# The second-choice additions at the ends of two expert layers, moved from VectorE to GpSimd

## The chip, the cores and the metric

The kernel runs on one core of one Trainium2 chip. The metric is the device time of one execution in microseconds, of which the median over several runs is taken. A profiled execution gives, beside its own time, a trace of every instruction; its span reaches from the first to the last instruction on the core.

## What is computed

The program is one forward pass of four residual layers over an input of 2 x 1024 tokens with 128 features: differential attention, a mixture of experts, attention with a decaying state, and the same mixture of experts again. Only the expert layer bears on this change:

```python
logits = xf @ router_w.T                       # 8 experts
scores = softmax(logits)
topk_scores, topk_ids = top_k(scores, 2)
topk_scores = topk_scores / topk_scores.sum(-1, keepdims=True)
for each expert (wg, wu, wd, w):
    h = silu(xf @ wg) * (xf @ wu)
    acc = acc + w[:, None] * (h @ wd)          # w is 0 but for the two chosen
x = x + acc
```

In words: x becomes x plus the first choice's result times its weight plus the second choice's result times its weight.

## The kernel before

`X` is the running x in on-chip memory: 128 partitions by 16 tiles of 128 values, fp32. It stays there through all four layers. Each layer writes one instruction list per engine inside a `Block`. At the end of a block every engine drains and meets the others at a barrier (L1234 in the records), after which GpSimd clears the semaphores (L2257 after the first expert layer, L2269 after the second) and a second barrier lets the next block begin.

`moe` is that expert layer, built twice: tag `m1` (after the first attention) and tag `m2` (the end of the program). It does not run every expert over every token. The tokens are sorted by expert into 39 slots of 128 rows. For each slot GpSimd gathers 128 rows with an indirect DMA (`gather`, L1274), TensorE, ScalarE and VectorE compute the expert's output `ys`, and GpSimd scatters its rows with an indirect DMA to `yd_rows` in HBM (`scatter`, L1280). That is 39 gathers and 39 scatters on GpSimd in a layer.

When all 39 scatters have landed (`results_in`, L1229 to L1232), the rows come back in token order: SyncE loads the first choices' rows, ScalarE's queue the second choices', each in four quarters of 4 tiles, into `GB` (printed `m_GB`; 128 x 512 values in a quarter). Then, by quarters q = 0 to 3:

- ScalarE multiplies the second choice's four tiles in place by their weights (L1407) and counts `weighted`.
- VectorE adds the first choice's four tiles times their weights to `X`, four instructions of 128x128 (L1507), and counts `first_added`.
- VectorE waits for both counts and adds the second choice's quarter to `X`, one instruction of 128x512 (L1513), and counts `summed`.

In the second layer SyncE waits for `summed` and stores each quarter of `X` to the output (L2265); it begins with that only when the first choice's last quarter has been loaded. In the first layer SyncE loads the next layer's weights instead (L2251 to L2254), and the next block begins with VectorE's statistics of `X` (L85).

The order within an engine's list is the order in which the code is written. VectorE's list at the end of the layer is L1507 x 4, L1513, four times over; GpSimd's list ends with the last scatter.

Of the kernel before, what the change touches and what calls it, by code (L numbers as in the profile page):

```python
# [9 lines left out]
ALU = mybir.AluOpType  # L10
# [1146 lines left out]
def moe(nc, tag, X, W3, ident, scratch, norm, route, statistics_done, deviations_done, experts_loaded, prefetch, store=None):  # L1157
# [4 lines left out]
    NQ, TQ = 4, 4  # L1162
# [7 lines left out]
    with ExitStack() as ctx:  # L1170
        def sb(name, shape, dt=F32):
            return ctx.enter_context(nc.sbuf_tensor(f"{tag}_{name}", shape, dt))
# [4 lines left out]
        def sems(names):  # L1177
            return [nc.alloc_semaphore(f"{tag}_{name}") for name in names.split()]
# [26 lines left out]
        GB = sb("GB", [P, NQ, 2, TQ, P])  # L1205
# [15 lines left out]
        weighted, first_added, summed = sems("weighted first_added summed")  # L1221
        NCONST = 8

        def quarter(q):
            return slice(TQ * q, TQ * q + TQ)
# [8 lines left out]
        with nc.Block() as block:  # L1234
            @block.sync
            def _(sp):
                for q in range(NQ):
                    sp.wait_ge(xn_ready, TQ * q + TQ)
                    sp.dma_start(XD[q * TQ * P:(q + 1) * TQ * P, :].rearrange("(t p) d -> p t d", p=P), XN[:, quarter(q), :])\
                      .then_inc(xn_stored, 16)  # L1240
                results_in(sp, 0)

                sp.wait_ge(gathered[NQ - 1][0], 16)
                prefetch(sp)
                if store is not None:
                    for q in range(NQ):
                        sp.wait_ge(summed, q + 1)
                        store(sp, q)

            @block.gpsimd  # L1250
            def _(pool):
# [26 lines left out]
                def scatter(s):  # L1278
                    pool.wait_ge(y_copied, s + 1)
                    pool.indirect_dma_start(out=YD[:, :], out_offset=bass.IndirectOffsetOnAxis(  # L1280
                        ap=target[:, s:s + 1], axis=0), in_=ys[:, s % YB], in_offset=None)\
                        .then_inc(ys_stored[s % YB], 16)
# [6 lines left out]
                for s in range(SLOTS):  # L1289
                    if s + XB < SLOTS:  # L1290
                        gather(s + XB)
                    scatter(s)

            @block.tensor
            def _(pe):


                def counts():
                    for t in range(NT):
                        nc.tensor.matmul(RC[:, (t + 1) * E:(NT + 1) * E].rearrange("p (t e) -> p t e", e=E), ones[:],  # L1300
                                         M[:, t:t + 1].to_broadcast([P, NT - t, E]), start=(t == 0), stop=False)
                        last = nc.tensor.matmul(RC[:, t * E:(t + 1) * E], tri[:], M[:, t], start=False, stop=(t == NT - 1))
                    last.then_inc(rc_done, 1)

                pe.wait_ge(const_c, 3)
                counts()

                order = [c for c in range(PC) if c >= PC // 2] + [c for c in range(PC) if c < PC // 2]
                for m, c in enumerate(order):
                    pe.wait_ge(placed, m + 1)  # L1310
                    planes = 3 if c >= PC // 2 else 2
                    for i in range(PI):
                        last = nc.tensor.matmul(IV[:, 0:planes * SLOTS].rearrange("p (a s) -> p a s", a=planes),  # L1313
                                                place_oh[:, c, :, i], marks[:, c, 0:planes, :, i],
                                                start=(m == 0 and i == 0), stop=(m == PC - 1 and i == PI - 1))
                last.then_inc(iv_done, 1)
                pe.wait_ge(experts_loaded, 48)

                def x_turn(s):
                    pe.wait_ge(xs_loaded[s % XB], s // XB * 16 + 16)  # L1320
                    if s:
                        pe.wait_ge(xt_copied, s)
                    nc.tensor.transpose(XT[:, 0:P], xs[:, s % XB], ident[:]).then_inc(xt_done, 1)  # L1323

                def up(s):
                    pe.wait_ge(w_copied, s + 1)
                    pe.wait_ge(xt_copied, s + 1)
                    for k, H, done in ((0, GP, g_done), (1, UP, u_done)):  # L1330
                        for j in range(FK):
                            last = nc.tensor.matmul(H[:, s % 2, j * P:(j + 1) * P], wgu[:, s % 2, k, j * P:(j + 1) * P],  # L1332
                                                    xt[:, s % 2], start=True, stop=True)
                        last.then_inc(done, 1)

                def down(s, e):
                    pe.wait_ge(h_ready, s + 1)
                    if s:
                        pe.wait_ge(y_copied, s)
                    for j in range(FK):  # L1340
                        last = nc.tensor.matmul(YP[:, 0:P], hs[:, s % 2, j * P:(j + 1) * P],  # L1341
                                                WD[:, bass.ds(e, 1), j, :].rearrange("p o d -> p (o d)"),
                                                start=(j == 0), stop=(j == FK - 1))
                    last.then_inc(y_done, 1)

                x_turn(0)
                pe.wait_ge(etab_ready, 1)
                up(0)
                x_turn(1)
                for s in range(SLOTS):  # L1350
                    e = pe.value_load(etab[0:1, s:s + 1], min_val=0, max_val=E - 1)
                    if s + 1 < SLOTS:
                        up(s + 1)
                    if s + 2 < SLOTS:
                        x_turn(s + 2)
                    down(s, e)
# [54 lines left out]
            def _(dve):  # L1411
# [92 lines left out]
                for q in range(NQ):  # L1504
                    dve.wait_ge(gathered[q][0], 16)
                    for t in range(TQ * q, TQ * q + TQ):
                        last = nc.vector.scalar_tensor_tensor(out=X[:, t, :], in0=GB[:, q, 0, t % TQ],  # L1507
                                                              scalar=wts[:, 0, t:t + 1], in1=X[:, t, :], op0=ALU.mult,
                                                              op1=ALU.add)
                    last.then_inc(first_added, 1)  # L1510
                    dve.wait_ge(weighted, TQ * q + TQ)
                    dve.wait_ge(first_added, q + 1)
                    nc.vector.tensor_tensor(X[:, quarter(q), :], X[:, quarter(q), :], GB[:, q, 1], ALU.add)\  # L1513
                      .then_inc(summed, 1)


def decay_attention(nc, X, ident, weights, LR, norm, route):
# [684 lines left out]
def program(nc, io, out, upto="all"):  # L2202
    NT = 16
    with ExitStack() as ctx:
# [51 lines left out]
        if upto != "attn_a":  # L2256
            with nc.cleanup_on_exit():  # L2257
                moe(nc, "m1", X, W3, ident, scratch, norm, route, NT // 2, 0, experts_loaded, load_decay_weights)
# [9 lines left out]
        if upto == "all":  # L2268
            with nc.cleanup_on_exit():  # L2269
                moe(nc, "m2", X, W3, ident, scratch, norm, route, NT, NT - 2, experts_loaded, lambda sp: None, store_out)  # L2270
# [28 lines left out]
```

## Time and profile before

| | us |
|---|---|
| median of 3 runs | 1130.73 (1129.43 to 1135.28) |
| profiled execution, its own time | 1133.65 |
| its span | 1131.9 |
| TensorE busy | 1006.1 (89%) |
| VectorE busy | 751.6 (66%) |
| ScalarE busy | 743.6 (66%) |
| GpSimd busy | 437.4 (39%) |

Busy times are sums over the span; they say how much an engine works, not which of them sets the end at a given place. The change touches two stretches, of some 8 us each, in which TensorE has nothing to do: the end of the first expert layer (about 632 to 641 us) and the end of the second, which is the end of the program (about 1121 to 1132 us). What counts there is the order in which loads land and VectorE, ScalarE and later GpSimd follow each other, which a timeline shows, and the barrier behind them, which needs the records of the sequencers (printed DVEq, POOLq, SPq).

### The profile page before, as it was taken

The numbers are of one execution on the slowest core, as the hardware profiler recorded it, in microseconds if no ns is written. First come the engines' busy times: TensorE is split into PE (matmuls) and PEld (weight loads), VectorE is DVE, ScalarE is ACT, GpSimd is POOL, SyncE is SP. The second block draws the span as 40 slices with busy tenths as digits, with TensorE's granted clock in tenths as the row PEclk, the third lists the DMA queues.
The fourth block names the chain that finished last, engine by engine and source line by source line (L and its number), as shares of the span: only waits on it lengthen the run. The fifth ranks groups of instructions, "written<-read, shape, count | busy, mean of one in ns | idle before, by whom it ended". The sixth has DMA issues, their size and how long they took to land. (4 is left out here: it accounts for less than half of the span.)

```text
span 1131.9 us, 26076 instructions
## 1 busy us (share of the span) xinstructions
PE 1006.1 (89%) x9820; PEld 691.3 (61%) x9820; DVE 751.6 (66%) x1519; ACT 743.6 (66%) x1496; POOL 437.4 (39%) x580
## 2 busy tenths in 40 slices
PE   5889999999999999748999489999999999479993
PEld 3333333333333334548999367888888888479993
DVE  7699999999999997882333635656566666443333
ACT  4658888887888887345665366676666666356663
POOL 3752112211122211217764124444444444256761
PEclk9889999999999999968999589999999999779997
DMA  2243111111111100611111422111212110021114
GB/s 71 84 126 100 31 31 49 39 31 30 31 47 42 31 2 3 223 38 48 48 48 36 157 70 76 39 76 39 75 39 68 45 65 12 8 64 49 50 41 126
DMA packets 40033, 64.65 MB, mean 57 GB/s; under 512 B 10024, under 2 KB 21032, under 8 KB 37992
## 3 DMA queue, kind: packets, MB, share of 16 engines
q1 hardware_dynamic: 31736, 50.14, 14.0%
q0 software_dynamic: 4992, 10.23, 3.4%
q10 hardware_dynamic: 3184, 2.63, 0.7%
q8 instruction: 81, 1.33, 0.5%
q14 instruction: 40, 0.33, 0.1%
HBM read 47.86 MB, written 14.68 MB: 55 GB/s over the span
## 5 line engine op out<-in xcount | busy, mean ns | idle before, releaser
L890 ACT ACTIVATE PB<-S 128x512 f32<-128x512 f32 x576 | 307.9, 597 | 71.3 <-PE S L696 66.5
L996 DVE TENSOR_REDUCE mx<-S 128x2 f32<-128x1024 f32 (+1 forms) x192 | 207.5, 1127 | 7.6 <-PE S L682 7.6
L958 POOL TENSOR_SCALAR_AFFINE_SELECT PB<-PB 128x512 f32<-128x512 f32 x128 | 79.0, 635 | 306.9 <-ACT PB L890 306.8
L731 PE MATMUL PV<-PB,VP 128*32 128x256 f32 (+2 forms) x2432 | 177.7, 379 | 0.0
L1489 DVE TENSOR_TENSOR m_hs<-m_gs,m_UP 128x512 f32<-128x512 f32 x78 | 53.7, 689 | 159.3 <-ACT m_gs L1380 157.2
L696 PE MATMUL S<-W 50*128 50x512 bf16 (+3 forms) x768 | 123.9, 328 | 4.9 <-ACT PB L890 4.2
L682 PE MATMUL S<-W 48*128 48x512 bf16 (+3 forms) x640 | 94.4, 326 | 13.4 <-DVE mx L992 4.9
L1280 POOL DMA_INDIRECT yd_rows<-m_ys,m_target x78 | 76.6, 981 | 59.9 <-DVE m_ys L1496 59.9
L1274 POOL DMA_INDIRECT m_xs<-xn_rows,m_source x78 | 75.8, 972 | 48.1 <-DVE m_source L1469 24.9
L731 PEld LDWEIGHTS PV<-PB,VP 128*32 128x32 f32 x2432 | 51.6, 108 | 69.1 <-issue 59.4
L682 PEld LDWEIGHTS S<-W 48*128 48x128 bf16 x640 | 26.8, 94 | 108.3 <-issue 44.7
L1332 PE MATMUL m_GP<-m_xt,m_wgu 128*128 128x128 f32 x624 | 84.8, 280 | 1.8 <-ACT m_xt L1376 1.8
L986 DVE TENSOR_REDUCE mx<-S 128x8 f32<-128x1024 f32 x64 | 78.3, 1223 | 11.6 <-PE S L675 11.2
L1332 PE MATMUL m_UP<-m_xt,m_wgu 128*128 128x128 f32 x624 | 84.1, 279 | 0.0
L1341 PE MATMUL m_YP<-W,m_hs 128*128 x624 | 82.6, 275 | 1.2 <-DVE m_ys L1496 1.2
L1386 ACT ACTIVATE m_wgu<-W 128x1024 f32 x78 | 82.6, 1058 | 1.4 <-issue 1.3
L1376 ACT ACTIVATE m_xt<-m_XT 128x128 f32<-128x128 f32 x78 | 21.6, 277 | 91.5 <-PE m_XT L1323 91.5
L1868 ACT ACTIVATE d_enegs<-d_PA 128x512 f32<-128x512 f32 x64 | 37.8, 590 | 64.6 <-PE d_PA L1667 60.2
L1332 PEld LDWEIGHTS m_GP<-m_xt,m_wgu 128*128 128x128 f32 x624 | 77.8, 196 | 3.1 <-issue 3.1
L1901 ACT ACTIVATE d_DM<-d_LQ,d_nL 128x128 f32<-128x128 f32 x252 | 78.1, 387 | 0.0
L1332 PEld LDWEIGHTS m_UP<-m_xt,m_wgu 128*128 128x128 f32 x624 | 77.7, 196 | 0.0
L1341 PEld LDWEIGHTS m_YP<-W,m_hs 128*128 128x128 f32 x624 | 75.8, 192 | 1.6 <-issue 1.6
(311 smaller groups left out, 1947.5 us busy)
## 6 DMA issues: line engine op xcount, KB each, us to landing
d_LQ<-l_rows SPq DMA_DIRECT2D x15, 1024.0 KB, 4.7
W<-qk_parts SPq DMA_DIRECT2D x210, 32.0 KB
qk_parts<-OT SPq DMA_DIRECT2D x24, 256.0 KB, 3.0
W<-qk_parts SPq DMA_DIRECT2D x30, 96.0 KB
W<-in_L_ffn_w_gate SPq DMA_DIRECT2D x1, 2048.0 KB, 9.3
W<-in_L_ffn_w_up SPq DMA_DIRECT2D x1, 2048.0 KB, 14.6
xn_rows<-m_XN SPq DMA_DIRECT2D x8, 256.0 KB, 2.3
m_GB<-yd_rows SPq DMA_DIRECT2D x8, 256.0 KB, 5.5
```

The costliest lines, as they stand in the source:

```text
L682: ins = nc.tensor.matmul(S1[:, b, a, 256 * k:256 * k + w], QS[base:base + KR, s, h, qb * P:(qb + 1) * P], KS[base:base + KR, s, h, c * 512 ...
L696: ins = nc.tensor.matmul(S2[:, j % 3, col:end], KS[base:base + KM, s, h, kb * P:(kb + 1) * P], QS[base:base + KM, s, h, q0:q0 + end - col] ...
L731: ins = nc.tensor.matmul(PV[32 * u:32 * u + 32, shift + col:shift + end], VP[:, g, kb, u // 2, :], PB[:, slot, col:end], start=(kb == 0 an ...
L890: nc.scalar.activation(PB[:, j % NPB, :], S2[:, j % 3, :], ACT.Exp, scale=SC).then_inc(exp_done, 1)
L958: nc.gpsimd.affine_select(out=tri, in_=tri, compare_op=ALU.is_ge, fill=0.0, base=0, pattern=[[0, U], [1, P]], channel_multiplier=-1).then_ ...
L986: nc.vector.reduce_max(mx[:, g % 2, 2].rearrange("p a h q -> p (a h) q")[:, :, q:q + 2], S1[:, b].rearrange("p a (h j k) -> p (a h) j k", ...
L996: nc.vector.reduce_max(mx[:, g % 2, c, :, heads[0], qb], S1[:, b, :, 0:w], AX.X)\
L1280: pool.indirect_dma_start(out=YD[:, :], out_offset=bass.IndirectOffsetOnAxis(ap=target[:, s:s + 1], axis=0), in_=ys[:, s % YB], in_offset= ...
L1332: last = nc.tensor.matmul(H[:, s % 2, j * P:(j + 1) * P], wgu[:, s % 2, k, j * P:(j + 1) * P], xt[:, s % 2], start=True, stop=True)
L1341: last = nc.tensor.matmul(YP[:, 0:P], hs[:, s % 2, j * P:(j + 1) * P], WD[:, bass.ds(e, 1), j, :].rearrange("p o d -> p (o d)"), start=(j ...
L1386: nc.scalar.activation(wgu[:, s % 2], W3[:, 0:2 * n].rearrange("p (k e f) -> p k e f", k=2, e=E) [:, :, bass.ds(e, 1), :].rearrange("p k o ...
L1901: last = nc.scalar.activation(DM[:, i, j % 2, j // 2], LQ[:, b, h], ACT.Exp, bias=nL[:, t, h:h + 1])
```

## The change

The addition of the second choice's quarter leaves VectorE's list and is written at the end of GpSimd's, after the last scatter, with the same two waits and the same count. It is done in both expert layers, four additions each.

```diff
                     scatter(s)
 
+                for q in range(NQ):
+                    pool.wait_ge(weighted, TQ * q + TQ)
+                    pool.wait_ge(first_added, q + 1)
+                    nc.gpsimd.tensor_tensor(X[:, quarter(q), :], X[:, quarter(q), :], GB[:, q, 1], ALU.add)\
+                      .then_inc(summed, 1)
+
             @block.tensor
...
                     last.then_inc(first_added, 1)
-                    dve.wait_ge(weighted, TQ * q + TQ)
-                    dve.wait_ge(first_added, q + 1)
-                    nc.vector.tensor_tensor(X[:, quarter(q), :], X[:, quarter(q), :], GB[:, q, 1], ALU.add)\
-                      .then_inc(summed, 1)
```

VectorE, end of the second layer, before (`m_hs` is the gated hidden value of a slot, `m_ys` the slot's output; from the third row on the end of the layer; two more pairs like the last two rows follow):

```order
L1489 TENSOR_TENSOR m_hs<-m_gs,m_UP 128x512
L1496 COPY m_ys<-m_YP 128x128 x2
L1507 SCALAR_TENSOR_TENSOR X<-m_GB,m_wts,X 128x128 x4
L1513 TENSOR_TENSOR X<-X,m_GB 128x512
L1507 SCALAR_TENSOR_TENSOR X<-m_GB,m_wts,X 128x128 x4
L1513 TENSOR_TENSOR X<-X,m_GB 128x512
```

VectorE at the same place, after (the diff shifts the line numbers by 6):

```order
L1502 COPY m_ys<-m_YP 128x128
L1495 TENSOR_TENSOR m_hs<-m_gs,m_UP 128x512
L1502 COPY m_ys<-m_YP 128x128 x2
L1513 SCALAR_TENSOR_TENSOR X<-m_GB,m_wts,X 128x128 x16
L1234 UNCONDITIONAL_BRANCH
```

VectorE's sixteen weighted additions now stand in one run, with waits only for the loads of their quarters.

GpSimd, end of the first layer, before (L1234 leaves the block, with its drain and barrier; L2257 clears the semaphores; L68 and L1596 belong to the next layer):

```order
L1274 DMA m_xs<-xn_rows,m_source 128x128
L1280 DMA yd_rows<-m_ys,m_target 9088x128 x9
L1234 UNCONDITIONAL_BRANCH
L2257 ISA
L68 UNCONDITIONAL_BRANCH
L1596 MEMSET d_ones 128x128
```

GpSimd at the same place, after:

```order
L1274 DMA m_xs<-xn_rows,m_source 128x128
L1280 DMA yd_rows<-m_ys,m_target 9088x128 x9
L1297 TENSOR_TENSOR X<-X,m_GB 128x512 x4
L1234 UNCONDITIONAL_BRANCH
L2259 ISA
L68 UNCONDITIONAL_BRANCH
L1598 MEMSET d_ones 128x128
```

The four additions stand between the last scatter and the block's end, so that GpSimd's drain comes behind them and no longer directly behind the last indirect DMA. At the end of the second layer its list changes in the same way. The lists of TensorE, ScalarE and SyncE are the same as before.

## Rows read from the trace of the kernel before

**Rows 1.** Page: the span, and the chain that ended last by engine

```profile
span 1131.9 us, 26076 instructions
...
PE 10%; DVE 1%; DMA 1%; POOL 0%; issue 0%; ACT 0%; POOLq 0%; DVEq 0%; ACTq 0%
```

**Rows 2.** Timeline, end of layer 2: start, duration, engine, line, operation [idle before]

```profile
1114.87 0.96 POOL L1280 DMA_INDIRECT yd_rows<-m_ys,m_target  x1 [0.78 <-DVE m_ys L1496]
1117.24 1.76 SPq L1232 DMA_DIRECT2D m_GB<-yd_rows  x4
...
1121.43 1.14 DVE L1507 SCALAR_TENSOR_TENSOR X<-m_GB,m_wts,X 128x128 f32<-128x128 f32 x4 [6.83 <-DMA m_GB<-yd_rows]
1121.63 2.55 ACT L1407 ACTIVATE m_GB<-m_GB,m_wts 128x128 f32<-128x128 f32 x8 [10.26 <-DMA m_GB<-yd_rows]
1122.94 0.69 DVE L1513 TENSOR_TENSOR X<-X,m_GB 128x512 f32<-128x512 f32 x1 [0.38 <-ACT m_GB L1407]
...
1126.18 1.28 ACT L1407 ACTIVATE m_GB<-m_GB,m_wts 128x128 f32<-128x128 f32 x4 [0.18 <-DMA m_GB<-yd_rows]
...
1128.48 0.69 DVE L1513 TENSOR_TENSOR X<-X,m_GB 128x512 f32<-128x512 f32 x1
```

**Rows 3.** Timeline, end of layer 1 and first work behind it

```profile
632.80 1.14 DVE L1507 SCALAR_TENSOR_TENSOR X<-m_GB,m_wts,X 128x128 f32<-128x128 f32 x4 [6.76 <-DMA m_GB<-yd_rows]
...
636.27 2.44 ACT L1407 ACTIVATE m_GB<-m_GB,m_wts 128x128 f32<-128x128 f32 x8 [0.60 <-DMA m_GB<-yd_rows]
...
639.90 0.69 DVE L1513 TENSOR_TENSOR X<-X,m_GB 128x512 f32<-128x512 f32 x1
...
641.63 3.19 DVE L85 BATCH_NORM_STATS2 d_ln_stats<-X 128x6 f32<-128x128 f32 x16 [1.04 <-PEq L2257]
```

**Rows 4.** Layer 2, first choice's loads of quarters 1, 2, 3: issue to landing

```profile
DMA to landing us min/median/max: 5.0/5.0/5.0
...
DMA to landing us min/median/max: 6.3/6.3/6.3
...
DMA to landing us min/median/max: 7.4/7.4/7.4
```

**Rows 5.** Three lines' instructions: duration ns min/median/max, first and last start, shapes

```profile
L1507 DVE SCALAR_TENSOR_TENSOR X<-m_GB,m_wts,X x32: 343/346/351, 632.8 to 1128.0; 128x128 f32<-128x128 f32 x32
...
L969 POOL TENSOR_TENSOR PB<-VP,rs x7: 1057/1060/1567, 467.7 to 483.0; 128x512 f32<-128x512 f32 x7
...
L1067 DVE TENSOR_TENSOR VP<-VP,y x16: 424/424/787, 431.8 to 477.5; 128x256 f32<-128x256 f32 x16
```

**Rows 6.** Timeline, two places where VectorE and GpSimd work at once

```profile
474.12 1.06 POOL L969 TENSOR_TENSOR PB<-VP,rs 128x512 f32<-128x512 f32 x1 [0.31 <-PE S L761]
...
474.67 0.79 DVE L1067 TENSOR_TENSOR VP<-VP,y 128x256 f32<-128x256 f32 x1
...
482.98 0.69 DVE L1126 TENSOR_TENSOR PB<-VP,rs 128x512 f32<-128x512 f32 x1
483.02 1.57 POOL L969 TENSOR_TENSOR PB<-VP,rs 128x512 f32<-128x512 f32 x1 [7.84 <-DVE rs L1085]
```

**Rows 7.** Drains at block ends: ns min/median/max, first and last start

```profile
L1234 POOLq DRAIN  x2: 7629/7638/7647, 626.1 to 1114.6; - x2
L1234 DVEq DRAIN  x2: 698/700/703, 639.9 to 1128.5; - x2
...
L1234 SPq EVENT_SEMAPHORE  x2: 17/17/17, 640.8 to 1129.9; - x2
...
L607 POOLq DRAIN  x1: 1674/1674/1674, 483.0 to 483.0; - x1
```

**Rows 8.** The last scatter's flight (chain), SyncE's last wait (waits), scatters (page)

```profile
1114.87 2.23 DMA yd_rows<-m_ys,m_target
...
SPq L2271 <- DMA out_x<-X: 0.8, 1, 0.8
...
L1280 POOL DMA_INDIRECT yd_rows<-m_ys,m_target x78 | 76.6, 981 | 59.9 <-DVE m_ys L1496 59.9
```

## The prediction, made before the changed kernel was run

> **What bounds the kernel now.** I began with the page: TensorE is busy for 89% of 1131.9 us, and the chain that ended last lies mostly on it [rows 1]. That says nothing of this change, since TensorE is idle at both places that the diff touches. So I went to the timeline of each place, then to the landing times of the loads, then to rows where GpSimd and VectorE work at once, and last to the drains and barriers that close each block.
>
> The reader should see three things. First, the end of layer 2 is VectorE's: from 1121.43 it runs four rounds of 1.14 us (L1507 x 4) and 0.69 us (L1513), and the last addition ends at 1128.48 + 0.69 = 1129.17; it waited for ScalarE only once, 0.38 us [rows 2]. ScalarE's weighting ends at 1126.18 + 1.28 = 1127.46, 1.7 us sooner. Layer 1 has the same shape, 632.80 to 640.59 [rows 3]. Second, behind the last addition stands a barrier. The engines pass it at 640.8 and 1129.9 [rows 7]; statistics of X follow at 641.63 [rows 3], and in layer 2 the clearing of semaphores and SyncE's wait for the last output store, 0.8 us [rows 8]. Third, GpSimd's drain at that barrier takes 7.63 and 7.65 us [rows 7]. It starts at 626.1 and 1114.6 and ends at about 633.75 and 1122.25, long before VectorE is done, so that today it costs nothing.
>
> **The additions themselves.** VectorE loses 8 instructions of 0.69 us, 5.5 us in all. GpSimd gains 8 two-input fp32 operations of 128x512; L969 is the same kind and shape, 1.06 us undisturbed [rows 5]. If nothing disturbed them, the last one would start when ScalarE's last weight is done, 1127.46 + 0.05 = 1127.51, and end at 1128.57: 0.60 us sooner than 1129.17. In layer 1 ScalarE ends at 636.27 + 2.44 = 638.71 [rows 3], the addition at 639.82, 0.77 us sooner. Together -1.4 us.
>
> But the two engines get in each other's way when both read two inputs from on-chip memory. L1067 takes 0.42 us as a rule and 0.79 us at its longest, which is where L969 is under way: L969 ends at 475.18 and L1067 at 475.46, 0.28 us behind it. The other way round, L969 takes 1.57 us when L1126 started 0.04 us before: L1126 ends at 483.67, L969 at 484.59, 0.92 us behind it [rows 5, 6]. So one waits until the other is done, and saves only some 0.14 us of its start. L1507 reads X and GB, the additions too. The Trainium skill, page "SBUF — State Buffer", section "Who interferes with whom", gives this as a rule: a VectorE instruction with two SBUF inputs and a GpSimd instruction that reads SBUF share an interface, and the second blocks until the first is done. By that rule, too, the case is not the -1.4 us of free running but the walk below; the trace agrees, with 0.37 and 0.51 us of waiting.
>
> The walk for layer 2, with loads of quarters 1 to 3 issued at 1117.6, 1118.1 and 1118.6 and landing at 1122.7, 1124.4 and 1126.0 [rows 2, 4]: VectorE begins quarter 1 at 1122.70. GpSimd is ready at 1122.96, when L1513 is today, gets in behind an instruction of VectorE and ends at 1124.02. An L1507 alone takes 0.35 us and four take 1.14 [rows 2, 5], so they start 0.26 apart; held up, the first ends 0.35 - 0.14 = 0.2 us after GpSimd. VectorE's three left end at 1124.02 + 0.20 + 2 x 0.26 = 1124.75. GpSimd's second addition follows VectorE's next instruction (until 1125.01) and ends at 1125.93; VectorE 1126.66 (its loads are there since 1124.4); third addition, again behind one instruction of VectorE, 1127.84; VectorE 1128.57; the last one, alone, 1128.62 to 1129.68. That is 0.5 us later than 1129.17. If VectorE's runs of four are never broken up, the same terms give 1129.6 to 1129.8. Fully one behind the other, 4 x 1.14 + 4 x 1.06 from 1121.43 with 0.2 us of handshakes, it is 1130.4, +1.2. The low end is the -0.6 above. I take +0.5 in either layer: last additions end at 1129.68 and 641.08.
>
> **The drain.** This is where the sum is decided. GpSimd's drain at L607 ends with the work before it: it starts at 483.0, takes 1.67 us and ends 0.1 us after L969, 484.59 [rows 6, 7]. The two of 7.6 us stand directly behind the indirect DMAs. The last of these is issued by 1114.87 + 0.96 = 1115.83 and has landed at 1117.10 [rows 2, 8], yet the drain ends at 1122.25, 5.15 us later, and the two differ by 18 ns. Nothing else in the profile lasts until then. I read it as work that the drain does itself once a block has indirect DMAs behind it: 39 gathers and 39 scatters in a layer [rows 8], and 7.63 / 78 is 98 ns for each. Behind the additions this work begins 14 us later than today, where nothing covers it: VectorE, ScalarE and SyncE wait at the barrier for GpSimd.
>
> Its price: a drain starts about 0.2 us before the instruction ahead of it runs (1114.6 against 1114.87). With the last addition from 1128.62 it would end at 1128.4 + 7.64 = 1136.1. From below: only the 5.15 us behind a landed DMA are its own, 1129.68 + 5.15 = 1134.8. From above: the whole 7.64 begins when the addition ends, 1137.3. I take 1136.1, which agrees with counting from the end of issue (1115.83 to 1122.25, 6.4 us). Against the barrier at 1129.85 this is +6.25; SyncE's 0.8 us for the last store are then covered, so +5.45 (4.2 to 6.7). In layer 1 the drain ends at 639.8 + 7.64 = 647.45, against 640.6 for VectorE's drain (639.9 + 0.70): +6.85 (5.6 to 8.1). Nothing that follows makes it up, as the next block needs X and the barrier.
>
> **Sum:** 5.45 + 6.85 = 12.3 us (9.8 to 14.8), with the lock's 0.5 us a layer in it. On the profiled execution that is 1133.65 + 12.3 = 1145.9. That execution lies 2.9 us above the median, which is scatter between runs (1129.43 to 1135.28), so I put the difference on the median: 1130.73 + 12.3 = 1143.0.
>
> **Rival 1, not slower: the drain is hidden.** Its 7.6 us run from the last indirect DMA, wherever the drain stands (entries taken off the ring while GpSimd waits, say). They would be over at 1122.25, before the first addition at 1122.96, and likewise in layer 1. For it: the drain at L607 has no work of its own. The Trainium skill's page "PSUM — Partial Sum Buffer", section "Engine vs sequencer instructions", says that a drain waits for its engine to be fully idle, and no more. By that rule GpSimd's drain would end with the last addition, and the time be as here; the 5.15 us after a landed DMA are not explained by it. Against: GpSimd stands idle 1.8 us of each 2.8 us round in the slots and could have cleared its backlog there. What remains is the lock, +0.5 us twice: 1131.7 us (up to 1133.1 if all is serial).
>
> **Rival 2, faster: free running.** Drain hidden, and the weighted additions do not block: -1.4, 1129.4 us. Rows 6 speak against it.
>
> **Rival 3, slower still:** the whole drain after the addition in both layers, plus serial additions (0.7 a layer more): 14.8 + 1.4, 1147 us.
>
> **Chances.** A measurement of this kernel can tell about 0.5%, 5.7 us. Drain exposed 0.58 (forecast 1143.0, own range 1139.5 to 1146.5), rival 3 0.05, rival 1 0.29, rival 2 0.06; 0.02 for a gain above 0.5% that I see no way to. So faster 0.02, same 0.35, slower 0.63. As the second case holds more than 0.2, the range must reach it: 1130.0 to 1147.0.
>
> **What would show it.** In the profile after: GpSimd's drain at L1234 (7.6 us, beginning near 640 and 1128) and the first statistics behind layer 1 near 648.5 instead of 641.63: the drain is right. A drain of about 1 us there and statistics near 642: rival 1. Additions of 1.06 us and weighted additions of 0.35 us all through: no lock; one of them near 1.2 us or an L1507 above 1 us: the lock. The last output store should be issued near 1129.7 in both cases; its landing would no longer end the program if the drain does. The forecast fails if the 7.6 us are bound to the last indirect DMA and not to the drain.

## The result, and the profile after

The changed kernel takes 1149.74 us (median of 4 runs, 1148.56 to 1152.25). The kernel before, run beside it, takes 1132.62 us (median of 4, 1129.43 to 1135.28; the three runs shown ahead are among them). The ratio is 1.0154, with a 95% interval of 1.013 to 1.0179: 14.7 to 20.3 us slower. The forecast was slower, by 12.3 us, and its range ended at 1147.0, 2.7 us too low.

The page of the changed kernel shows a span of 1146.8 us and, but for GpSimd's 10 us more, busy times within 1.3 us of those before. VectorE's is no shorter although 5.5 us of additions have left it, since an instruction that is held up counts as busy:

```profile
span 1146.8 us, 26076 instructions
...
PE 1006.1 (88%) x9820; PEld 691.8 (60%) x9820; DVE 752.9 (66%) x1511; ACT 743.7 (65%) x1496; POOL 447.8 (39%) x588
```

Busy times do not tell where the time went. The timeline of layer 1's end does (start, duration, engine, line, operation, idle time before it); it answers to [rows 3]:

```profile
629.16 1.14 DVE L1513 SCALAR_TENSOR_TENSOR X<-m_GB,m_wts,X 128x128 f32<-128x128 f32 x4 [6.78 <-DMA m_GB<-yd_rows]
...
630.51 6.38 DVE L1513 SCALAR_TENSOR_TENSOR X<-m_GB,m_wts,X 128x128 f32<-128x128 f32 x12 [0.20 <-DMA m_GB<-yd_rows]
630.78 1.27 POOL L1297 TENSOR_TENSOR X<-X,m_GB 128x512 f32<-128x512 f32 x1 [7.15 <-ACT m_GB L1413]
...
632.87 1.26 POOL L1297 TENSOR_TENSOR X<-X,m_GB 128x512 f32<-128x512 f32 x1 [0.82 <-DVE X L1513]
...
634.95 1.26 POOL L1297 TENSOR_TENSOR X<-X,m_GB 128x512 f32<-128x512 f32 x1 [0.82 <-DVE X L1513]
...
637.03 1.26 POOL L1297 TENSOR_TENSOR X<-X,m_GB 128x512 f32<-128x512 f32 x1 [0.82 <-DVE X L1513]
...
646.12 3.19 DVE L85 BATCH_NORM_STATS2 d_ln_stats<-X 128x6 f32<-128x128 f32 x16 [9.23 <-PEq L2259]
```

The last addition ends at 638.29, 9.13 us after the first weighted addition began; before it was 7.79. Then 7.8 us pass in which no engine does anything, until the statistics start. What fills them is in the records of the barrier (name, count, ns min/median/max, first and last start), which answer to [rows 7]:

```profile
L1234 DVEq DRAIN  x2: 3367/3409/3451, 633.5 to 1134.3; - x2
L1234 SPq DRAIN  x2: 122/123/124, 636.4 to 1139.5; - x2
L1234 POOLq DRAIN  x2: 7737/7744/7750, 637.0 to 1137.7; - x2
L1234 SPq EVENT_SEMAPHORE  x2: 17/17/17, 645.2 to 1145.6; - x2
```

GpSimd's drain starts with the last addition (637.0) and ends at 644.8, 6.46 us behind the end of that addition. SyncE passes the barrier at 645.2. Layer 2 is the same: 1137.7 + 7.74 = 1145.4, barrier at 1145.6.

The kernel can be cut into stretches that are compared one by one: from the first weighted addition of layer 1 to the first statistics behind it (end 1), from there to the first weighted addition of layer 2, and from there to the end of the span (end 2).

| us | end 1 | end 2 | sum over before |
|---|---|---|---|
| before | 8.83 | 10.47 | |
| before, on the second chip | 8.84 | 10.46 | |
| changed | 16.96 | 16.77 | 14.4 |
| changed, second profile | 16.94 | 16.93 | 14.6 |
| early drain | 10.47 | 11.82 | 3.0 |
| late drain, additions on VectorE | 15.42 | 15.70 | 11.8 |
| drain in the middle as well | 12.96 | 12.83 | 6.5 |
| first layer only | 16.87 | 10.50 | 8.1 |
| second layer only | 8.83 | 16.80 | 6.3 |

The two ends repeat within 0.2 us from profile to profile, on two chips. They are the measure of the mechanism. The rest of the program, which the change does not touch, moves as well: in the changed kernel's profile the stretch ahead of end 1 is 3.6 us shorter than before (629.16 against 632.80) and the one between the ends 4.1 us longer. With the 14.4 us of the ends that makes the 14.9 between the two spans.

### The profile page after: what moved, and what is told of

It reads as the page before. It is cut to its first block and busy times, and to the rows that moved or that the text cites. A ratio compares the mean times of both kernels' runs of the same rounds, so it can differ in the third digit from the quotient of the medians.

```text
span 1146.8 us, 26076 instructions
## 1 busy us (share of the span) xinstructions
PE 1006.1 (88%) x9820; PEld 691.8 (60%) x9820; DVE 752.9 (66%) x1511; ACT 743.7 (65%) x1496; POOL 447.8 (39%) x588
## 6 DMA issues: line engine op xcount, KB each, us to landing
W<-in_L_ffn_w_up SPq DMA_DIRECT2D x1, 2048.0 KB, 14.6
```

## The experiments

**The changed kernel once more**, for scatter.

> The changed kernel once more, beside the others on the same chip, to tell which part of the +17 us is the two ends of the layers and which part is the clock elsewhere. Theory: ends of the layers cost 8.1 us (first weighted addition of layer 1 to first statistics behind it: 8.83 us before, 16.96 in the changed kernel) and 6.3 us (first weighted addition of layer 2 to the end: 10.47 and 16.77); the 4.1 us more between them go with TensorE's granted clock (0.97 against 0.99 there) and change from run to run. Rival: those 4.1 us come again in each run, as a longer idle stretch in front of the third layer keeps the clock low for longer.

Measured: ratio 1.0136 (1.0102 to 1.0169) to 1134.49 us, so 11.6 to 19.2 us slower; ends 16.94 and 16.93 us. The additions took 1.26 us again. So what the ends lose is the change's, 14.5 us of the 17.1 in the first comparison. The 4.1 us between the ends came again here (483.8 us against 479.8), which by itself would speak for the rival; the kernel before once more, at the end of this section, shows how far.

**An early drain.** One more drain, directly behind the last scatter, in the changed kernel:

```diff
                     scatter(s)
+                nc.gpsimd.drain()
 
                 for q in range(NQ):
                     pool.wait_ge(weighted, TQ * q + TQ)
```

> The changed kernel with one more GpSimd drain directly behind the last scatter, ahead of the four additions, in both layers. Theory (the drain works through the indirect DMAs behind it, once): the added drain takes 7.6 us, ends near 7.4 us after the last scatter's start, some 0.7 us before the first addition is ready, and so costs nothing; the drain at the block's end then takes only as long as the last addition, about 1.3 us. What is left of the loss is the additions on GpSimd: 1.34 us in layer 1, 1.23 in layer 2 by the two traces, plus 0.3 for a barrier that GpSimd reaches last: 2.5 to 3.5 us slower than before, 1135 us against 1132. Rival (a drain behind a block with indirect DMAs always costs its 6.4 us, whatever drains stood before): the block's drain stays at 7.7 us and the kernel at +15 to +17 us. Rival (the GpSimd additions themselves make the drain long): the added drain is short, the last one stays long, +15 to +17 us.

Measured: ratio 1.004 (1.002 to 1.006) to 1134.49 us, 2.3 to 6.8 us slower. L1293 is the added drain, L1234 the one at the block's end:

```profile
L1293 POOLq DRAIN  x2: 7637/7642/7647, 623.3 to 1114.9; - x2
```

```profile
L1234 POOLq DRAIN  x2: 1349/1349/1349, 637.9 to 1129.2; - x2
```

The 7.64 us have moved to the new drain, which ends at 631.0 and 1122.5, before the first additions (631.70 and 1122.95). The last drain is as long as the addition ahead of it and 0.09 us more. The ends lose 1.6 and 1.35 us instead of 8.1 and 6.3. Both rivals fall: the work is done once, and it is not the additions that make it.

**A late drain alone.** The kernel before, with one wait more on GpSimd; all additions stay on VectorE:

```diff
                     scatter(s)
+                pool.wait_ge(summed, NQ)
```

> The kernel before, all additions on VectorE; GpSimd only waits at the end of its list until all four quarters are summed, so that its drain begins when VectorE is done. Theory (late drain alone makes the loss): GpSimd's drain begins near the last addition's end and takes 6.4 to 7.7 us; the barrier comes 6.5 to 7.5 us later in layer 1, and the program's end 5.5 to 6.5 us later in layer 2 (0.8 us of the wait for the last store is covered): +12 to +14 us against before, and the additions on VectorE stay at 0.69 us. Rival (the loss comes from the additions on GpSimd and the lock between the engines): +0 to +1 us. Rival (the drain's work is over while GpSimd waits): drain under 0.2 us, +0 to +0.5 us.

Measured: ratio 1.0076 (1.005 to 1.0103), 5.7 to 11.7 us slower. The ends lose 6.6 and 5.2 us, 11.8 together: a little below the 12 to 14 that I wrote, as nothing but the drain's own work is left in it. The whole time moved by less than I expected too, and its interval ends just under what the ends lose. The drain alone, with no instruction of GpSimd under way ahead of it:

```profile
L1234 POOLq COMPARE_BRANCH  x2: 38/38/38, 642.0 to 1137.1; - x2
L1234 POOLq DRAIN  x2: 6414/6421/6428, 642.2 to 1137.2; - x2
```

VectorE's last addition starts at 641.29 and takes 0.69 us; GpSimd passes its wait at 642.0, drains until 648.6, and the statistics start at 649.61. So the larger part of the loss needs no addition on GpSimd at all.

**A drain in the middle**, to see what its length hangs on. The changed kernel, with a drain behind scatter 19:

```diff
                     scatter(s)
+                    if s == 19:
+                        nc.gpsimd.drain()
```

> The changed kernel with one more GpSimd drain in the middle of the slots, behind scatter 19 (28 gathers and 20 scatters issued by then, 11 gathers and 19 scatters after it), in both layers; looked at for its drains. Theory (so much for each indirect DMA since the last drain, 6.4 to 7.6 us for 78, 82 to 98 ns each): the drain in the middle takes some 4 to 5 us, the last one 30 x 82 to 98 ns = 2.5 to 2.9 us beyond the end of the last addition. Rival (a fixed time when any indirect DMA lies behind it): both take 6.4 to 7.6 us. The whole time is then that of the changed kernel less up to 4 us a layer at the end, plus what the drain in the middle holds up, which the slots' slack may hide in part.

Measured: one profile, span 1138.7 us. L1294 is the drain in the middle:

```profile
L1294 POOLq DRAIN  x2: 5204/5210/5217, 574.8 to 1067.7; - x2
```

```profile
L1234 POOLq DRAIN  x2: 3812/3812/3812, 640.6 to 1133.5; - x2
```

The last one less the 1.35 us that cover the addition is 2.46 us for 30 indirect DMAs: 82 ns each. The late drain's 6.42 us for 78 are 82 ns each, and the changed kernel's 7.74 - 1.35 = 6.39 as well. The drain in the middle follows 48, 3.94 us at that price, and starts 1.22 us before the scatter ahead of it is issued (574.83 and 576.05): 5.16 us, against 5.20 and 5.22, a little over the 4 to 5 expected. A fixed time is ruled out, and so is a length that grows with the time since the last drain: the late drain starts 16 us later than that of before (642.2 against 626.1) and does the same 6.4 us of work. The drain's length is proportional to the indirect DMAs issued since the last drain. Each of them moves 128 rows, so whether the price is for a DMA or for its rows is not told apart, and what the drain does in that time no trace shows. The drain of before fits too: 0.23 us ahead of the last scatter, 0.96 of its issue and 6.42 make 7.61 us, against 7.63 and 7.65 [rows 2, 7]. In this sum the scatter's landing has no part.

**One layer at a time.** These and the two runs below went to another chip, on which the kernel before takes 1171.1 us (19 runs); TensorE waits more for ScalarE's copies in the slots there, and the ends are unchanged (table). The edit, for the first layer (`store` is None there); the second has the condition turned round:

```diff
-                for q in range(NQ):
+                for q in range(NQ if store is None else 0):
...
                     last.then_inc(first_added, 1)
+                    if not (store is None):
+                        dve.wait_ge(weighted, TQ * q + TQ)
+                        dve.wait_ge(first_added, q + 1)
+                        nc.vector.tensor_tensor(X[:, quarter(q), :], X[:, quarter(q), :], GB[:, q, 1], ALU.add)\
+                          .then_inc(summed, 1)
```

> Additions on GpSimd in the first expert layer only; the second is as before. By the traces so far the end of layer 1 (first weighted addition to first statistics behind it) is 16.96 us instead of 8.83, the end of layer 2 is 10.47 as before: +8.1 us, of which drain and barrier 6.8 and additions with the lock 1.3. Rival (a late drain costs only where other work waits behind it, so one layer carries nearly all): +12 to +16 here and under +3 in the run with the second layer only. The stage between the layers: if its 4 us more come with the longer idle stretch ahead of it, they stand here (GpSimd's last d_YN of that stage 332 us behind the first statistics, 329 before) and not in the run with the second layer only.

> Additions on GpSimd in the second expert layer only. End of layer 2 (first weighted addition to the end of the span) 16.8 us instead of 10.47: +6.3 us; end of layer 1 8.8 us as before. If the 3 us in the third layer come with the change in layer 1, d_YN's last start is 329 us behind the first statistics, as before; if they are chance of the clock or of the kernel's code, it is 331 to 332 here as well.

Measured: first layer only 1.006 (1.0033 to 1.0086) to 1171.1 us, 3.9 to 10.1 us slower; second only 1.0055 (1.0031 to 1.008), 3.6 to 9.4. The ends lose 8.0 and 0.0, and 0.0 and 6.3 us. Each layer pays its own share and they add up.

**What the additions on GpSimd collide with.** As the early drain, but VectorE's first additions take their second operand from PSUM:

```diff
-                                                              scalar=wts[:, 0, t:t + 1], in1=X[:, t, :], op0=ALU.mult,
+                                                              scalar=wts[:, 0, t:t + 1], in1=UP[:, 1, 0:P], op0=ALU.mult,
```

> As e1 (drain ahead of the additions), but VectorE's first additions take their second operand from PSUM, so that they read one tensor from on-chip memory instead of two. What they add is then not X, so this part of the computation is left out. Theory (two-input reads of both engines exclude each other): GpSimd's additions keep 1.26 us, but VectorE's sixteen instructions take 0.35 us all through, with no 1.4 us one among them, and the last addition starts when ScalarE's last weight is done: from the first weighted addition to the last addition's end 7.3 to 7.6 us instead of 9.1, under the 7.74 of before. Rival (GpSimd at work slows VectorE in any case, or the 2.08 us from one addition to the next is set by semaphores and not by the lock): 2.08 us between additions as in e1, 9 us in all.

Measured: one profile. The same two lines with two operands in on-chip memory (early drain), then with one:

```profile
L1514 DVE SCALAR_TENSOR_TENSOR X<-m_GB,m_wts,X x32: 337/344/1401, 630.1 to 1128.7; 128x128 f32<-128x128 f32 x32
...
L1298 POOL TENSOR_TENSOR X<-X,m_GB x8: 1259/1262/1266, 631.7 to 1129.2; 128x512 f32<-128x512 f32 x8
```

```profile
L1514 DVE SCALAR_TENSOR_TENSOR X<-m_GB,m_wts,m_UP x32: 339/340/347, 647.9 to 1165.5; 128x128 f32<-128x128 f32 x32
...
L1298 POOL TENSOR_TENSOR X<-X,m_GB x8: 1261/1266/1269, 649.5 to 1166.2; 128x512 f32<-128x512 f32 x8
```

No instruction of VectorE is held up any more (at most 347 ns against 1401), and GpSimd's additions take 1.27 us, as good as the 1.26 with the lock. In layer 2 the timeline has the additions wait for ScalarE alone:

```profile
1160.15 1.12 DVE L1514 SCALAR_TENSOR_TENSOR X<-m_GB,m_wts,m_UP 128x128 f32<-128x128 f32 x4 [6.75 <-DMA m_GB<-yd_rows]
...
1164.91 2.57 POOL L1298 TENSOR_TENSOR X<-X,m_GB 128x512 f32<-128x512 f32 x2 [0.54 <-ACT m_GB L1414]
```

From first weighted addition to last addition it is 7.33 us, against 9.07 with the lock and 7.74 before. In layer 1 it is 7.21, against 9.11 and 7.79. So the exclusion hangs on VectorE's second read from on-chip memory. The Trainium skill's page "SBUF — State Buffer", section "Who interferes with whom", has this as a rule: a VectorE instruction with two SBUF inputs contends with a GpSimd instruction that reads SBUF. The trace agrees, with 1401 ns against 347; a GpSimd instruction with a single input was not tried. What the lock costs here is 1.7 us in layer 2 and 1.9 in layer 1, and additions on GpSimd free of it would end only 0.4 and 0.6 us sooner than those on VectorE did.

**The kernel before once more**, with its own profile.

> The kernel before once more, with its own profile, to see how far its stretches change from run to run: ends of the layers 8.8 and 10.5 us in any case; the third layer's last d_YN 329 us behind the first statistics if its length is the kernel's own, up to 332 us if the clock's dips come by chance.

Measured: ends 8.84 and 10.46 us, and the third layer's last d_YN (GpSimd's normalised output, written once in each of that layer's 16 rounds) starts 330.8 us behind the first statistics, not 329.0; with one layer changed it is 330.6 in either run. Nearly all of the 1.8 us lie in one round of that layer, and TensorE's granted clock (the column behind POOL's busy time) tells the rounds apart. The stretch before that round, the round, and all the rest, first in the profile of before, then in this one, then in the changed kernel:

```profile
641.60:690.60 49.00, 43.71 (x261) 34.85 (x261) 26.53 (x90) 31.59 (x66) 13.96 (x27) 0.80 0.23 87
690.60:709.60 19.00, 18.91 (x171) 15.64 (x169) 11.06 (x24) 12.66 (x30) 9.15 (x14) 1.00 0.16 57
709.60:970.80 261.20, 257.83 (x2308) 213.67 (x2306) 161.48 (x411) 168.03 (x400) 123.12 (x175) 1.00 0.14 50
```

```profile
664.60:713.70 49.10, 44.76 (x260) 35.82 (x260) 26.45 (x90) 31.59 (x66) 13.81 (x26) 0.77 0.23 88
713.70:734.40 20.70, 20.60 (x171) 16.89 (x171) 11.25 (x24) 12.66 (x30) 9.30 (x15) 0.92 0.15 52
734.40:995.50 261.10, 257.73 (x2306) 213.53 (x2306) 161.50 (x411) 168.03 (x400) 123.02 (x175) 1.00 0.14 50
```

```profile
646.10:695.10 49.00, 44.13 (x260) 35.26 (x260) 26.52 (x90) 31.59 (x66) 13.97 (x27) 0.78 0.18 62
695.10:717.10 22.00, 21.91 (x171) 17.73 (x170) 11.25 (x24) 12.65 (x30) 9.13 (x14) 0.86 0.14 50
717.10:978.30 261.20, 257.82 (x2308) 213.60 (x2306) 161.53 (x411) 168.06 (x400) 123.10 (x175) 1.00 0.13 50
```

The same 171 matmuls take 19.0 us at a granted clock of 1.00 of 2.4 GHz, 20.7 at 0.92 and 22.0 at 0.86; the stretches around it are equal within 0.1 us. Cut finer, the changed kernel's round has one piece at the lower level, 0.50, which is 1.2 GHz:

```profile
695.00:701.00 6.00, 6.00 (x35) 4.51 (x36) 2.40 (x5) 0.00 (x0) 2.94 (x3) 0.50 0.02 4
```

Six microseconds at half the clock are the 3 us. In the 3 us ahead of it (692 to 695) TensorE was busy for 1.12 us. The kernel before has the same lull: in its second profile 1.21 us busy out of 3 (711 to 714), with 0.50 behind it from 715 to 718, and in its first 1.43 (687 to 690), with 1.00 behind it. So the dip is in the unchanged kernel too, and it is not the change alone that makes it. That the first profile of before has none is what makes 3.0 us of the 4.1 look like the change's. Whether the change makes the dip more often or longer (2.9 and 3.0 us in both profiles of the changed kernel, 1.8 in this one) stays open: that wants many profiles of each. It does not follow the idle stretch ahead of the layer, as the rival had it: with an end 1 of 10.47 us (early drain) the last d_YN starts 331.7 us behind the statistics, with 15.42 (late drain) 330.7, with 16.87 (first layer only) 330.6. Of the other 1.1 us, 1.0 lies between that last d_YN and the first gather of the second expert layer: 28.7 us in the changed kernel, 27.7 in the first profile of before and 26.0 in its second, so that this too moves without the change.

## Why the prediction was right or wrong

**The place and the cause: right.** The loss sits where the forecast had it: GpSimd's drain, until then covered by VectorE, does its work at the barrier. The step rested on one reading, that the 7.6 us of [rows 7] end 5.15 us after the last DMA has landed while another drain ends with its engine's work, and on the count of 78. The early drain, the late drain and the one in the middle each bear it out. That it is a price for each DMA was a guess from a single count; only the drain in the middle, with 48 and 30, made it more than that. Rival 1 fell with the first profile after, by the sign that the prediction named (a drain of 7.7 us at 637.0 and 1137.7). By the Trainium skill's page "PSUM — Partial Sum Buffer", section "Engine vs sequencer instructions", a drain waits for its engine to be idle; behind indirect DMAs the measurement decides otherwise, with 6.4 us of drain (late drain) in which the profile shows no instruction of GpSimd.

**The drain's size: right.** I took 6.4 us behind the last addition, from the end of the last scatter's issue; it measured 6.45 and 6.46, and 6.42 alone. The price of one DMA is 82 ns, not 98: I had divided the whole record, with the issue ahead of it, by 78.

**The step that was mis-sized: the additions.** The walk gave +0.5 us a layer; it measured +1.34 (9.13 against 7.79) and +1.23 (8.97 against 7.74), 1.6 us more in all. One term of it was wrong: an addition takes 1.26 us, not the 1.06 of L969. L969's second operand is a small tensor repeated (`rs` broadcast over 16 values), while the additions read two full ones. L946 was at hand in the same trace with 1.15 (its second operand is bf16). The cause of the difference was not tried. Four times 0.20 us is 0.8, nearly the whole miss of a layer. The rest of the round was about right: from one addition's end to the next one's the walk had 1.91 us (1124.02 to 1125.93), and it measured 2.08, of which 0.82 pass until the next record starts. The lock itself held as drawn, as a rule with one L1513 passing ahead of each addition and three behind it. My upper bound of +1.2, all serial, was computed with 1.06 as well and so too low.

**What was left out: the barrier.** From the last drain's end to the statistics behind layer 1 it is 0.99 us before (640.64 to 641.63) and 1.36 in the changed kernel (644.75 to 646.12), 0.3 to 0.4 us that the sum did not have. It is not that GpSimd comes last: in the late drain it does too, and there it is 1.00 us (648.61 to 649.61). All six profiles with the additions on GpSimd in layer 1 have 1.30 to 1.37, the four others 0.99 to 1.01. In layer 2 there is none of it: from GpSimd's drain to the end of the span it is 1.35 us in the changed kernel and 1.36 in the late drain. The cause stays open.

**The sum.** Forecast 6.85 and 5.45, measured 8.1 and 6.3 us: 14.4 against 12.3, inside the 9.8 to 14.8 given for the difference. Of the 2.1 us that the sum was short, 1.6 are the additions, 0.3 the barrier and 0.2 the drain. The range for the time failed on the other half of it. It stood on a median of three runs, 1130.73; with one run more the kernel before is at 1132.62, and with thirteen, on the first experiments' chip, at 1134.49. 1132.62 + 14.4 is 1147.0, the range's very edge. I had taken 2.9 us between the profiled execution and the median as scatter that would not count, and then left the upper end no room for it. The remaining 2.7 us to 1149.74 lie in the comparison's interval (14.7 to 20.3 us). They come from outside the ends, where nothing was changed and where one pair of profiles differs by -3.6 and +4.1 us; how much of them the dips of the clock make is not shown.

**The last store: right.** It is issued with the last addition and no longer ends the program: SyncE waits 6.1 us for the barrier instead (before, 0.8 us for the store, [rows 8]):

```profile
SPq L1234 <- PEq L1234: 6.1, 1, 6.1
```

## What to carry to other kernels

Before work is put at the end of an engine's list, look at the records of the barrier behind it: a drain that costs nothing today may only be covered by another engine, and work put ahead of it makes it start later without making it shorter. If GpSimd has issued indirect DMAs, give it a drain directly behind the last of them, where waiting is free, before it gets other work. And a two-input elementwise operation given to GpSimd beside two-input work on VectorE is not done in parallel; it queues, and is dearer than the one it replaces (1.26 against 0.69 us here). The best version with the additions on GpSimd (early drain) is still 0.4% slower than the kernel before, and no other variant of the whole computation did better.

## What the runs showed of the hardware that was not expected

- A drain of GpSimd costs 82 ns for each indirect DMA issued since its last drain: 6.42 us for 78, 2.46 for 30, none for 0 (early drain: 0.09 us longer than the addition). GpSimd's idle time does not shorten it: in the late drain it sat idle for 13.6 us behind the last scatter, and the drain kept its whole length.
- An addition of two full fp32 tensors of 128x512 takes GpSimd 1.26 us, with VectorE held up or not; only layer 2's first one, which starts beside an instruction of VectorE, takes up to 1.43. The same operation type with a broadcast operand takes 1.06.
- When both engines want their second read, GpSimd gets it between two of VectorE's queued instructions: one passes, the next is held for 1.4 us instead of 0.35, until the addition is done.
